# Experts' stages after half chunks, y on ScalarE, four x1 buffers, another order at the end

## The reference, cut to what matters

```python
    out = out.transpose(0, 2, 1, 3).reshape(bsz, q_len, HEADS * HEAD_DIM)   # 8 x 100 x 4096
    x1 = x + tanh(g_xattn[0]) * (out @ Wo)                                  # 8 x 100 x 1024
...
    flat = _layernorm(x1)                       # the kernel's y: (x1 - mean) / sqrt(var + 1e-5)
    logits = flat @ router_w.T + router_b       # 8 experts
    topv, topi = top_k(softmax(logits), 2)
    gates = topv / sum(topv)
    h = einsum('nd,erd->ner', flat, A)          # 8 experts x rank 16 = 128 columns
    out2 = einsum('ner,eor->no', h * w[:, :, None], Bm) * (8.0 / 16)
    return x1 + tanh(g_ffn[0]) * out2
```

## Time and profile before

| | us |
|---|---|
| median of three executions | 1753.11 |
| lowest and highest | 1750.63, 1757.34 |
| the profiled execution, its own time | 1748.85 |
| its span in the profile | 1746.9 |
| start of chunk 16 in it | 1539.05 |
| end of the last chunk in it | 1701.1 |
| DVE's last instruction ends | 1742.8 |

### The profile page before, as it was taken

The page is one execution under the profiler, slowest core; times in us unless marked ns, Lnnn a source line. Parts: engine busy times, 40 slices in busy tenths (PEclk is TensorE's granted clock), DMA queues, the critical chain, the costliest instruction groups (busy, mean ns, idle before and its releaser), DMA issues.

```text
span 1746.9 us, 26303 instructions
## 1 busy us (share of the span) xinstructions
PE 1692.9 (97%) x9312; PEld 1508.2 (86%) x9312; DVE 1170.6 (67%) x2074; ACT 879.1 (50%) x1655; POOL 730.5 (42%) x584
## 2 busy tenths in 40 slices
PE   7999999999999999999999999999998999999996
PEld 6788888678888879999999999999997888999994
DVE  6778876777777733777777777777766664455546
ACT  5455554454544423666666666666656654343321
POOL 1444543234443402666666666666665550000000
PEclk9999999999999999999999999999999999999999
DMA  5567778545566554344444333444444654665522
GB/s 193 163 185 237 231 213 247 140 145 173 158 176 161 138 214 144 120 122 123 131 130 123 119 122 120 131 131 130 127 126 160 207 181 160 218 218 191 194 102 66
DMA packets 215654, 278.13 MB, mean 159 GB/s; under 512 B 51956, under 2 KB 187956, under 8 KB 210020
## 3 DMA queue, kind: packets, MB, share of 16 engines
q1 hardware_dynamic: 214948, 269.90, 49.7%
q10 hardware_dynamic: 576, 6.55, 0.9%
HBM read 189.77 MB, written 86.64 MB: 158 GB/s over the span
## 4 chain that ended last, share of the span: by engine, by line
PE 87%; DVE 5%; ACT 3%; issue 2%; DMA 2%; POOL 0%; SPq 0%; DVEq 0%; ACTq 0%; POOLq 0%
PE bank L757 26%; PE bank L759 25%; PE bank L758 25%; PE bank L895 5%; PE bank L862 2%; PE bank L791 1%; DVE mx L1652 1%; PE bank L1045 1%; DMA at_raw<-at_d 1%; DMA kT<-kT_d 1%; DVE wo_lo L1672 1%; ACT w_hi L1111 1%; DVE pT_lo L1646 1%; DMA wr<-Wkv 0%; ACT pT_hi L1286 0%
## 5 line engine op out<-in xcount | busy, mean ns | idle before, releaser
L739 POOL TENSOR_SCALAR pr<-pr,rr 100x461 f32<-100x461 f32 x256 | 382.8, 1501 | 299.0 <-DVE rr L1667 299.0
L757 PE MATMUL bank<-w_hi,a_hi 128*128 128x512 f32 (+1 forms) x856 | 340.7, 398 | 12.2 <-DVE a_lo L1442 9.3
L759 PE MATMUL bank<-w_hi,a_lo 128*128 128x512 f32 (+1 forms) x856 | 334.9, 391 | 0.0
L758 PE MATMUL bank<-w_lo,a_hi 128*128 128x512 f32 (+1 forms) x856 | 334.3, 391 | 0.0
L1295 ACT ACTIVATE pr<-bank,nm,rq 100x461 f32<-100x461 f32 x256 | 188.6, 737 | 170.9 <-DVE nm L1658 167.8
L1652 DVE TENSOR_REDUCE mx<-bank 100x1 f32<-100x461 f32 x256 | 161.7, 632 | 81.4 <-PE bank L759 76.1
L757 PEld LDWEIGHTS bank<-w_hi,a_hi 128*128 128x128 f32 (+1 forms) x856 | 157.8, 184 | 49.5 <-issue 10.4
L759 PEld LDWEIGHTS bank<-w_hi,a_lo 128*128 128x128 f32 (+1 forms) x856 | 157.5, 184 | 38.0
L757 PE MATMUL bank<-xT_hi,wq_hi 128*128 128x400 f32 x512 | 188.2, 368 | 0.5 <-issue 0.5
L757 PE MATMUL bank<-at_hi,wo_hi 128*128 128x400 f32 x512 | 183.1, 358 | 5.7 <-DVE at_lo L1683 2.9
L758 PEld LDWEIGHTS bank<-w_lo,a_hi 128*128 128x128 f32 (+1 forms) x856 | 158.0, 185 | 34.8
(11 more groups left out here) (133 smaller groups left out, 3496.1 us busy)
## 6 DMA issues: line engine op xcount, KB each, us to landing
wo_raw<-Wo SPq DMA_DIRECT2D x32, 1024.0 KB, 4.9
kT_d<-kst SPq DMA_DIRECT2D x56, 512.0 KB, 5.2
v_d<-vst SPq DMA_DIRECT2D x56, 512.0 KB
at_raw<-at_d SPq DMA_DIRECT2D x32, 800.0 KB, 7.2
kT<-kT_d SPq DMA_DIRECT2D x64, 361.0 KB, 4.7
kvr<-ctxT SPq DMA_DIRECT2D x44, 512.0 KB, 5.8
wq_raw<-Wq SPq DMA_DIRECT2D x32, 512.0 KB, 6.0
vv<-v_d SPq DMA_DIRECT2D x64, 240.0 KB
```

Of the source, the lines that this page charges most:

```text
L739: pool.tensor_scalar(pr[0:NQ, u % 2, i], pr[0:NQ, u % 2, i], rr[0:NQ, i:i + 1], None, ALU.mult).then_inc(p_done, 1)
L757: pe.matmul(o, lh, rh, start=start, stop=False, skip_group_check=more)
L758: pe.matmul(o, lh, rl, start=False, stop=False, skip_group_check=more)
L759: return pe.matmul(o, ll, rh, start=False, stop=stop, skip_group_check=more)
```

## The change

It has five parts, all in the stretch from chunk 16 on.

- **Stages after half chunks.** The loop runs over 32 half chunks n (half chunk n belongs to chunk 16 + n // 2; two heads, 24 matmuls). The five stages of batch t (t = 0 to 3) stand behind half chunks 7t, 7t + 2, 7t + 3, 7t + 5 and 7t + 6 (the table `FFN_AT`). All of batch 3, `up(3)` and `final(3)` too, is now done before the last chunk.
- **SP's list.** The loads of the chunks, `load_res` and `store` are written into the same table: `load_res(t + 2)` with its wait for `residual(t)` stands at n = 7t + 2, `store(t - 1)` at n = 7t + 3.
- **y by ACT.** DVE's `norm` is gone; ACT makes y as `Identity(x1 * rstd - mean * rstd)`, for which POOL makes two more small values (-mean, then -mean x rstd) and counts one more semaphore.
- **x1 in four buffers.** `residual(t)` waits for `final(t - 4)`.
- **The end's order.** The third and fourth batch of the end (6 and 7) are turned out before the low rank product of batch 4, and the rest is interleaved anew.

```diff
+FFN_AT = {7 * t + a: (t, i) for t in range(B // 2) for i, a in enumerate((0, 2, 3, 5, 6))}
...
-        x1 = at("x1", HI + 38400, [P, 3, D])
+        x1 = at("x1", HI + 38400, [P, 4, D])
...
-            for c in range(2 * G):
-                t = c // 4
-                load_chunk(2 * G + c)
-                if c % 4 == 0 and t >= 1:
-                    sp.wait_ge(x1_done, 2 * t)
-                    load_res(t + 1)
-                if c % 4 == 3 and t >= 1:
-                    store(t - 1)
-            for t in range(TB - 1, B):
-                if t + 2 < B:
+            for n in range(4 * G):
+                if n % 2 == 0:
+                    load_chunk(2 * G + n // 2)
+                t, i = FFN_AT.get(n, (0, 0))
+                if i == 1:
                     sp.wait_ge(x1_done, 2 * t + 2)
                     load_res(t + 2)
-                if t >= TB:
+                if i == 2 and t >= 1:
                     store(t - 1)
...
             for t in range(B):
                 pool.wait_ge(ag2_done, t + 1)
                 pool.tensor_scalar(mv2[0:NQ, t, 0:1], mv[0:NQ, t, 1:2], 1.0, LN_EPS, ALU.mult, ALU.add).then_inc(va2_done, 1)
-                pool.wait_ge(va2_done, t + 1)
-                pool.tensor_tensor(mv2[0:NQ, t, 1:2], mv2[0:NQ, t, 0:1], mhalf[0:NQ, 0:1], ALU.pow).then_inc(rs2_done, 1)
+                pool.tensor_scalar(mv2[0:NQ, t, 2:3], mv[0:NQ, t, 0:1], -1.0, 0.0, ALU.mult, ALU.add).then_inc(va2_done, 1)
+                pool.wait_ge(va2_done, 2 * t + 2)
+                pool.tensor_tensor(mv2[0:NQ, t, 1:2], mv2[0:NQ, t, 0:1], mhalf[0:NQ, 0:1], ALU.pow).then_inc(va3_done, 1)
+                pool.wait_ge(va3_done, t + 1)
+                pool.tensor_tensor(mv2[0:NQ, t, 3:4], mv2[0:NQ, t, 2:3], mv2[0:NQ, t, 1:2], ALU.mult).then_inc(rs2_done, 1)
...
-            for c in range(2 * G):
-                t = c // 4
-                if c % G == 0:
-                    accumulators_free(1, c // G)
-                chunk(2 * G + c, between=(lambda: up(t - 1)) if c % 4 == 0 and t else None)
-                (turn_out, turn_y, low_rank, turn_h)[c % 4](t)
-            up(TB - 1)
+            stages = (turn_out, turn_y, low_rank, turn_h, up)
+            for n in range(4 * G):
+                if n % (2 * G) == 0:
+                    accumulators_free(1, n // (2 * G))
+                for i in range(2):
+                    chunk_head(2 * G + n // 2, n % 2 * 2 + i)
+                if n in FFN_AT:
+                    stages[FFN_AT[n][1]](FFN_AT[n][0])
...
+            def norm(t):
+                act.wait_ge(rs2_done, t + 1)
+                if t >= 2:
+                    act.wait_ge(t2_done, t - 1)
+                act.activation(y[0:NQ, t % 2], x1[0:NQ, t % 4], ACT.Identity, bias=mv2[0:NQ, t, 3:4],
+                               scale=mv2[0:NQ, t, 1:2]).then_inc(y_done, 1)
...
+            for n in range(4 * G):
+                m = 2 * G + n // 2 + 1
+                t, i = FFN_AT.get(n - 1, (0, None))
+                if i == 1:
+                    turned_y(t)
+                if i == 3:
+                    turned_h(t)
+                if i == 2:
+                    exps2(t)
+                if n - 2 in FFN_AT and FFN_AT[n - 2][1] == 0:
+                    norm(FFN_AT[n - 2][0])
                 if m < 4 * G:
-                    chunk_weights(m)
...
+                    (chunk_heads if n % 2 else chunk_weights)(m)
...
-                if t >= 3:
-                    dve.wait_ge(x2_done, 2 * (t - 3) + 2)
+                if t >= 4:
+                    dve.wait_ge(x2_done, 2 * (t - 4) + 2)
...
+                if i == 0:
+                    residual(t)
+                if i == 2:
+                    route_top(t)
+                if i == 4:
+                    final(t)
                 if m < 4 * G:
-                    chunk_weights(m)
...
+                    (chunk_heads if n % 2 else chunk_weights)(m)
+                if i == 2:
+                    route_gates(t)
```

More of the change, by code:

```diff
@@ L357, in build @@
         va2_done = sem("va2_done")
+        va3_done = sem("va3_done")
         rs2_done = sem("rs2_done")
@@ L634, in _ @@
                 load_chunk(m)
-            for c in range(2 * G):
-                t = c // 4
-                load_chunk(2 * G + c)
-                if c % 4 == 0 and t >= 1:
-                    sp.wait_ge(x1_done, 2 * t)
-                    load_res(t + 1)
-                if c % 4 == 3 and t >= 1:
-                    store(t - 1)
-            for t in range(TB - 1, B):
-                if t + 2 < B:
+            for n in range(4 * G):
[3 more added lines that the diff above has]
+                if i == 1:
                     sp.wait_ge(x1_done, 2 * t + 2)
                     load_res(t + 2)
-                if t >= TB:
+                if i == 2 and t >= 1:
                     store(t - 1)
-            store(B - 1)
+            store(TB - 1)
+            for t in range(TB, TB + 2):
+                sp.wait_ge(x1_done, 2 * t + 2)
+                load_res(t + 2)
+            for t in range(TB, B):
+                store(t)
             sp.wait_ge(x2_stored[0], 16 * B // 2)
@@ L998, in _, with chunk @@
                 values(UNITS - 1, t)
-            def chunk(m, between=None):
+            def chunk(m):
                 for i in range(R):
                     chunk_head(m, i)
-                    if between and i == R // 2 - 1:
-                        between()
             def accumulators_free(th, nh):
@@ L1829, in _ @@
             accumulators(0, 1)
-            for c in range(2 * G):
-                t, m = c // 4, 2 * G + c + 1
-                if c % 4 == 1:
+            for n in range(4 * G):
+                m = 2 * G + n // 2 + 1
+                t, i = FFN_AT.get(n - 1, (0, None))
+                if i == 0:
                     residual(t)
-                if c % 4 == 3:
+                if i == 2:
                     route_top(t)
+                if i == 4:
+                    final(t)
                 if m < 4 * G:
-                    chunk_weights(m)
-                if c % 4 == 1:
-                    norm(t)
-                if c % 4 == 3:
+                    (chunk_heads if n % 2 else chunk_weights)(m)
+                if i == 2:
                     route_gates(t)
-                if m < 4 * G:
-                    chunk_heads(m)
-                if c % 4 == 0 and t:
-                    final(t - 1)
-                if c % G == G - 1:
-                    accumulators(1, c // G)
-            def route(t):
-                route_top(t)
-                route_gates(t)
+                if n % (2 * G) == 2 * G - 1:
+                    accumulators(1, n // (2 * G))
             a, b, c, d = range(TB, B)
-            for do, t in ((residual, a), (final, a - 1), (norm, a), (residual, b), (route_top, a), (norm, b),
-                          (route_gates, a), (residual, c), (route, b), (norm, c), (final, a), (residual, d),
-                          (final, b), (norm, d), (route, c), (route, d), (final, c), (final, d)):
+            for do, t in ((residual, a), (residual, b), (residual, c), (route_top, a), (route_gates, a), (residual, d),
+                          (route_top, b), (route_gates, b), (final, a), (route_top, c), (route_gates, c), (final, b),
+                          (route_top, d), (route_gates, d), (final, c), (final, d)):
                 do(t)
```

41 lines of the change are left out of this document (12 added, 29 removed).

## The result

The change takes 1775.68 us (median of 4 runs, 1771.94 to 1778.77), against 1752.71 us of the kernel before on the same chip (4 runs): ratio 1.0126, 95% interval [1.0098, 1.0155]. It is slower by 23.0 us, where 15 us (to 1768) had been forecast.

A forecast was written before the change was run, and what follows sets the result against it. PE, busy for 97% of the span, was taken as the bound. Terms 13.8 + 3.3 + 1.8 + 2.0 - 4.2 gave +16.7 us: 1765.6 or 1769.8 by basis, forecast 1768, range 1756 to 1777.

The forecast's parts named there:

- Step 1: Chunks 21 and 28: loads stand behind SP's wait for x1, so PE waits 6.9 us each time, 13.8 in all.
- Step 2: Granted clock falls to 1.2 GHz around the two long PE waits, costing 1.65 us each, 3.3 in all.
- Steps 3 and 4: Small waits, mainly at batches 0 and 2, cost 1.8 us; batch 3's turn_h and up moving into the chunks, 2.0.
- Step 5: After the last chunk: PE's new list takes 37.5 us against 41.7, a gain of 4.2 us.
- Short waits: Rival: loads behind x1 land faster, PE waits 4.3 us twice; +8.4 us in all, 1757 to 1761; chance 0.15.
- the covered hold: Rival: SP's wait for x1 costs nothing and the end's gain remains; -2.2 us, 1748 to 1751; chance 0.07.
- The end gives nothing: Rival: slow clock and POOL's and ACT's new steps leave the end 0 to -2 us; 1770 to 1775; chance 0.10.
- The rule on 10 of 16 engines: A 100-partition xr transfer uses 10 of 16 DMA engines, holding them 1.6 us; would add 0.4 us per such load.

The follow-up runs named there:

- e2: Kernel before with only SP's wait for x1 and load_res of batches 1 and 3 moved ahead of the loads of chunks 22 and 30; 1772.86 us, ratio 1.0121.
- e1: The change with only SP's list altered: wait for x1 with load_res at half chunk 7t + 6, store at 7t + 5; 1753.02 us, ratio 1.0013.
- e5: The change with SP's wait for x1 moved later, and ACT making y of batches 1 and 3 behind at_hi; 1751.70 us, ratio 0.9990.
- e9: Kernel before with constants' transfers issued later, the new end order and four x1 buffers; batch 3's stages still at the end; 1744.24 us, ratio 0.9949.
- e7: The change with SP's waits for x1 kept, but the xr transfer issued behind the following chunk's load; 1772.53 us, ratio 1.0107.
- e4: The change with SP's wait for x1 moved later and the old end order on PE, DVE and ACT; 1758.32 us, ratio 1.0048.

## Why the prediction came out as it did

**Right in its mechanism.** SP's wait for x1 ahead of chunks 21 and 28 was named as the loss, with its two places on PE, y first and at_lo behind it; e2 shows it alone (+19.8 in the stretch) and e1 shows it gone.

**Step 1, the hold: 6.9 forecast, 8.3 measured, twice.** Ready was taken at 17.3 after half chunk 7; it was 18.7 (1589.79 to 1608.53), and PE would have wanted chunk 21 at 10.4 as forecast. This is the step that was mis-sized, by its term for the landing after x1: 8.6, measured 9.85, above the 9.1 that was its upper bound. That bound took the worst row at hand, a load behind an xr, and the 8.6 leaned on "no other load is in flight". Here SP had more to catch up on: a store and the next chunk's load were issued right behind, all within 1.6 us. On the profile the waits are 5.6 for y and 1.7 for at_lo, where 4.3 and 2.6 had been forecast: y waits for the whole lateness of the transfer, and the turning between the two waits, at half speed, fills 0.9 of the second.

**Step 2, the clock: 1.65 forecast, 1.8 measured, twice.** The level was right (0.50), and so was its length behind the start of chunk 21, 4.1 us where 3.4 to 4.2 had been taken. The clock had fallen 6 us before that, inside the wait, which the forecast didn't say. The turning of y at half speed cost nothing, since at_lo was not there yet.

**Steps 3 and 4, the small ones and batch 3's stages: 3.8 forecast, about 6 measured.** The small waits for at_lo are 2.0 in the change (5.4 less the two of 1.69), as forecast (1.8), and batch 3's stages are 2.0. The rest, 1.5 to 2 us, was in no term; about 1 of it is in e1 and e5 as well, and none of it was traced. e1's own 6.1 is made up otherwise: 2.8 of it is y ahead of at_hi in ACT's list at chunks with half a chunk of slack, which the prediction saw only within the hold, where it is covered by the transfer.

**Step 5, the end: -4.2 forecast, -4.6 in the profile.** The walk met its stations within 0.4 us (its own terms up to the first y add up to 7.4, as measured, where 7.7 was written). The same end took 35.6 to 37.1 in the five profiles that have it. The prediction did not say that the order pays only with batch 3's stages out of the end, which e9 showed.

The sum of the profile, 20.0 + 6.0 - 4.6 = +21.4, lies just above the upper bound of +21.2, where +16.7 had been forecast. From the 1753.11 of the shown median it gives 1774.5, beside 1775.68 measured. The forecast of 1768 had split the difference between that basis and the profiled execution's. That 1775.68 is inside the range of 1756 to 1777 is owed to the 2 to 3 us added for spread: the bounds of the sum ended at 1774.

**The rivals.** Short waits and the covered hold are out by the 9.0 us landing. "The end gives nothing" would have given nearly the measured time, 1770 to 1775, for another reason; the end's 37.1 rules it out as the cause.

**The rule on 10 of 16 engines** ("DMA: Bandwidth & Descriptors" of the Trainium skill, section "Why a DMA increments its semaphore by 16 and not by 1"): by the estimate it would have added 0.4 per hold. The trace agrees with the ten engines. In e1, with nothing but an xr in flight, the window reads:

```profile
1714.00:1714.50 0.50, 0.00 (x0) 0.00 (x0) 0.50 (x2) 0.00 (x0) 0.42 (x2) 1.00 0.66 254
```

The two numbers at the end are the mean busy share of the 16 DMA engines and GB/s: 0.66 and 254, where the change's load shows 0.97 and 406 (the window from 1603, above). At 254 GB/s an xr is 1.6 us, as estimated. How much of that falls on the load behind it is not told apart: no run here changed the partitions of xr, and e7 puts all that an xr ahead costs at 1.0 and 2.1 us of waiting.

## What to carry to other kernels

An in-order queue that issues loads is itself an engine with a list: a wait for a late result, put ahead of a load with 3 us of reserve, costs the whole chain behind it (10 us here, twice), however small the transfer that waits. Put such waits behind the loads that are due next, and look in the same way for transfers that nobody needs soon ahead of ones that somebody does (7 us here). Reordering an end pays only if every engine's list, not only TensorE's, is free for it: either half of the work alone (e4, e9) left the end at 43.1 and 40.7, where it was 41.4 to 43.1 before, and both together brought it to 35.6 to 37.1.
